# One band's PSUM read to ScalarE, the sums ahead of the differences' low halves on VectorE, and the row differences on GpSimd

## The chip, the core and the metric

One core of a Trainium2 chip runs the whole kernel. The metric is the device time of one execution in microseconds (us). TensorE (PE in the profile) multiplies, VectorE (DVE) and ScalarE (ACT) do the elementwise work and read PSUM, GpSimd (POOL) does elementwise work in SBUF, SyncE (SP) issues the transfers. PEld is TensorE's loading of weights.

## The reference, cut to what matters

The input is `x` of 8 images, 64 channels, 224 x 224, in fp32. With `g = _gn(x)` (group normalisation) the kernel returns

```python
res = conv3x3(g, W_id, b_id)                      # all 8 images: by far the largest part
out = leaky_relu(conv3x3(dmt, W_enc, b_enc), .01) # dmt comes from image 0 alone (wavelets, attention)
return x + (out + res)
```

`out` is one 64 x 224 x 224 map that is added to each image. The change concerns only `res` and the additions around it, which is the last stage of the kernel; the statistics, the wavelets and the `dmt` convolution run ahead of it.

## The kernel before

In the last stage an image is cut into an upper and a lower half, which lie on partitions 0 to 63 and 64 to 127, and each half into 14 bands of 8 rows. Of the 14 bands 7 are **direct** (a plain 3x3 convolution) and 7 are **minimal** (the F(2,3) scheme over rows, which makes two output rows from four products in place of six). Products run in fp16 with a high and a low half of each operand. That makes 56 direct bands and 56 minimal ones. The stage is written as 56 **rounds** `q`; in a round TensorE multiplies direct band `q+1` and minimal band `q` in turns, while the other engines prepare what the next rounds need. Each engine runs its list in order; semaphores join the lists.

TensorE's order in a round: `first_direct(q+1)`, `product_m2(q)`, `middle_direct(q+1)`, `product_m1(q)`, `last_direct(q+1)`, `product_m0(q)`, `product_m3(q)`, all on line L1766. `product_m0` waits for `b_seeded`, which VectorE's `seed_odd` gives.

What the names stand for, with the lines of the kernel before:

- `neighbour_sums(j)` (VectorE, L1928 and L1929): two operations of 896 columns on the raw band of minimal `j`; waits until that band's load has landed.
- `differences(j)` (VectorE, L1935): subtracts row r+2 from row r of that band in place, 1792 columns, fp32.
- `diffs_high` (ScalarE, L1863) and `diffs_low` (VectorE, L1946): high and low fp16 halves of the differences. `sums_high` (ScalarE, L1871) and `sums_low` (VectorE, L1940): the same for the sums.
- `high` and `full` (ScalarE, L1606 and L1612) and `split` (VectorE, L1619): the same for a direct band, 2240 columns.
- `read_direct(j, g)` (VectorE, L1954): reads bank pair `g` (0 or 1) of direct band `j` from PSUM into the stage for the store; `seed_direct` (ScalarE, L1633) then fills that bank for the next band. `seed_odd` (VectorE, L1961), `odd_rows` (VectorE, L1969), `even_rows` (ScalarE, L1886), `seed_minimal` (ScalarE, L1893) and `double` (ScalarE, L1879) do the minimal bands' work on PSUM.
- `build_part` (VectorE, L1734, L1738, L1743, L1745): makes half of the next image's weights. It runs in two of an image's seven rounds, for all images but the last: 14 **build rounds**.

The bands of `x` rotate through three buffers `xs`. SyncE's list in a round is: four stores of direct `q` (after both its banks are read), four stores of minimal `q-1`, then two loads of 560 KB each for direct `q+3`, then two for minimal `q+2`. A load waits for the buffer:

```python
def load(sp, k):
    ...
    if k >= XS:
        sp.wait_ge(split_done, k - XS + 1)
```

`split_done` is raised by `split` and by `diffs_low`. The load of minimal band `q+2` waits for `split(q+2)` in round `q`; the band is first read by `neighbour_sums(q+2)` in round `q+1`. GpSimd in this stage only fills border rows (L2019 and L2024).

Of the kernel before, what the change touches and what calls it, by code (L numbers as in the profile page):

```python
# [8 lines left out]
ALU = mybir.AluOpType  # L9
# [16 lines left out]
R = 8  # L26
NB = HALF // R
RH = R + 2
# [1417 lines left out]
def main(nc, x, t, out, ps, psum, sb, sem, top, pool_of, early, e_map, partner, mv_all, norm_all, w_max, unit):  # L1446
# [3 lines left out]
    with ExitStack() as s5:  # L1450
# [71 lines left out]
        banks_set = sem(top, "banks_set")  # L1522
        g_seeded = sem(top, "g_seeded")
        g_done = sem(top, "g_done")
        g_read = sem(top, "g_read")
        a_seeded = sem(top, "a_seeded")
        m2_done = sem(top, "m2_done")
        twice_ready = sem(top, "twice_ready")
# [30 lines left out]
        def place_w(j):  # L1559
            return min(2 * j + 2, ND + NW - 1)  # L1560
# [67 lines left out]
        def seed_direct(act, j, g):  # L1628

            i, b = direct(j)  # L1630
            if j:
                act.wait_ge(g_read, 2 * j - 1 + g)
            act.activation(g_bank[g], e_rows[:, :, b, g, :, :].rearrange("p r q w -> p r (q w)"), ACT.Identity,  # L1633
                           scale=lane(r_out, i), bias=lane(mean_r, i)).then_inc(g_seeded, 1)

# [192 lines left out]
        def sync(sp):  # L1828
            def store(i, b, p):
                for s in range(2):  # L1830
                    for k in range(2):
                        row0 = HALF * s + R * b + 4 * k
                        sp.dma_start(out[i, :, row0:row0 + 4, :].rearrange("c h w -> c (h w)"),
                                     stage[p][C * k:C * k + C, s, :, :].rearrange("c g n -> c (g n)")).then_inc(stored[p], 16)

            def store_direct(j):
                sp.wait_ge(g_read, 2 * j + 2)
                store(*direct(j), 0)

            def store_minimal(j):  # L1840
                sp.wait_ge(even_read, j + 1)
                sp.wait_ge(odd_read, 2 * j + 2)
                store(*minimal(j), 1)

            load(sp, 3)
            load(sp, 4)
            for q in range(NW):
                store_direct(q)
                if q:
                    store_minimal(q - 1)  # L1850
                load(sp, 2 * q + 5)
                load(sp, 2 * q + 6)
            store_minimal(NW - 1)
            for p in range(2):
                sp.wait_ge(stored[p], 64 * ND)

        def scalar(act):
            def diffs_high(j):
                i, b = minimal(j)
                act.wait_ge(diffs_ready, j + 1)  # L1860
                if j:
                    act.wait_ge(odd_done, j)
                act.activation(v_hi[:, 0:R, 1:1 + W], xs[place_w(j) % XS][:, 0:R * W].rearrange("p (r w) -> p r w", w=W), ACT.Identity,  # L1863
                               scale=norm_all[:, i, 0:1]).then_inc(diffs_hi, 1)

            def sums_high(j):
                i, b = minimal(j)
                act.wait_ge(sums_ready, j + 1)
                if j:
                    act.wait_ge(m1_done, j)  # L1870
                act.activation(v_hi[:, R:VR, 1:1 + W], sums.rearrange("p (r w) -> p r w", w=W), ACT.Identity,  # L1871
                               scale=norm_all[:, i, 0:1]).then_inc(sums_hi, 1)

            def double(j):
                i, b = minimal(j)
                act.wait_ge(m2_done, j + 1)
                if j:
                    act.wait_ge(b_seeded, j)
                act.activation(twice, a_bank, ACT.Identity, scale=-2.0, bias=lane(mean_r2, i)).then_inc(twice_ready, 1)  # L1879

            def even_rows(j):
                i, b = minimal(j)
                act.wait_ge(even_done, j + 1)
                if j:
                    act.wait_ge(stored[1], 64 * j)
                act.activation(stage[1][:, :, :, 0:W], a_bank.rearrange("p r (g w) -> p r g w", g=2), ACT.Identity,  # L1886
                               scale=lane(m_out, i)).then_inc(even_read, 1)

            def seed_minimal(j):
                i, b = minimal(j)  # L1890
                if j:
                    act.wait_ge(even_read, j)
                act.activation(a_bank.rearrange("p r (g w) -> p r g w", g=2), e_rows[:, :, b, :, 0, :], ACT.Identity,  # L1893
                               scale=lane(r_out, i), bias=lane(mean_r, i)).then_inc(a_seeded, 1)

            act.wait_ge(banks_set, 2)
            for q in range(-1, NW):
                if q >= 0:
                    diffs_high(q)
                if q >= 0 and q + 2 < ND:  # L1900
                    high(act, q + 2)
                if q >= 0:
                    double(q)
                if q >= 0 and q + 2 < ND:
                    full(act, q + 2)
                if q + 2 < ND:
                    seed_direct(act, q + 2, 0)
                if q + 1 < NW:
                    sums_high(q + 1)
                if q >= 0:  # L1910
                    even_rows(q)
                if q + 1 < NW:
                    seed_minimal(q + 1)
                if q + 2 < ND:
                    seed_direct(act, q + 2, 1)

        def vector(dve):
            def neighbour_sums(j):

                i, b = minimal(j)  # L1920
                k = place_w(j)
                landed(dve, k)
                if b == BOTTOM:
                    dve.wait_ge(filled, fill_of(i, b))
                v = xs[k % XS].rearrange("p (r w) -> p r w", w=W)
                odd, even = v[:, 1:R:2, :], v[:, 2:R + 1:2, :]
                half = [sums[:, CH * W * h:CH * W * h + CH * W].rearrange("p (r w) -> p r w", w=W) for h in range(2)]
                dve.scalar_tensor_tensor(half[0], odd, lane(neg_two, i), even, ALU.add, ALU.add)  # L1928
                dve.tensor_tensor(half[1], even, odd, ALU.subtract).then_inc(sums_ready, 1)  # L1929

            def differences(j):

                v = xs[place_w(j) % XS]
                dve.wait_ge(sums_ready, j + 1)
                dve.tensor_tensor(v[:, 0:R * W], v[:, 0:R * W], v[:, 2 * W:RH * W], ALU.subtract).then_inc(diffs_ready, 1)  # L1935

            def sums_low(j):
                i, b = minimal(j)
# [7 lines left out]
                dve.scalar_tensor_tensor(v_lo[:, 0:R, 1:1 + W], xs[place_w(j) % XS][:, 0:R * W].rearrange("p (r w) -> p r w", w=W),  # L1946
                                         norm_all[:, i, 0:1], v_hi[:, 0:R, 1:1 + W], ALU.mult, ALU.subtract).then_inc(split_done, 1)

            def read_direct(j, g):
                i, b = direct(j)  # L1950
                if j:
                    dve.wait_ge(stored[0], 64 * j)
                dve.wait_ge(g_done, 2 * j + g + 1)  # L1953
                dve.tensor_scalar(stage[0][:, :, g, :], g_bank[g], lane(m_out, i), None, ALU.mult).then_inc(g_read, 1)  # L1954

            def seed_odd(j):
                dve.wait_ge(m1_done, j + 1)
# [15 lines left out]
            for q in range(-1, NW):  # L1973
                if q > 0:
                    odd_rows(q - 1)
                if q >= 0:
                    diffs_low(q)
                if q + 1 < NW:
                    neighbour_sums(q + 1)
                i, b = direct(q + 1) if q + 1 < ND else (B, 0)  # L1980
                if i + 1 < B and b in DIRECT[2:4]:
                    build_part(dve, i + 1, DIRECT.index(b) - 2)
                if q + 1 < ND:
                    read_direct(q + 1, 0)
                if q >= 0 and q + 2 < ND:
                    split(dve, q + 2)
                if q >= 0:
                    seed_odd(q)
                if q + 1 < NW:
                    differences(q + 1)  # L1990
                    sums_low(q + 1)
                if q + 1 < ND:
                    read_direct(q + 1, 1)
            odd_rows(NW - 1)

        def tensor(pe):
# [14 lines left out]
        def gpsimd(pool):  # L2011
            for buf in (v_hi, v_lo):
                pool.memset(buf[:, :, 0:1], 0.0).then_inc(v_pads_set, 1)
                pool.memset(buf[:, :, WP - 1:WP], 0.0).then_inc(v_pads_set, 1)

            def fill_top(i):
                k = place_d(len(DIRECT) * i)
                pool.wait_ge(split_done, k - XS + 1)
                pool.memset(xs[k % XS][up, 0:W], 0.0).then_inc(filled, 1)  # L2019

            def fill_bottom(i):
                k = place_w(len(MINIMAL) * i + len(MINIMAL) - 1)
                pool.wait_ge(split_done, k - XS + 1)
                pool.tensor_copy(xs[k % XS][dn, (RH - 1) * W:RH * W], mean[dn, i:i + 1].broadcast_to((C, W))).then_inc(filled, 1)  # L2024

            for i in range(B):
                if i + 1 < B:
                    fill_top(i + 1)
                fill_bottom(i)

        ahead = Ahead(load=load, weights_load=weights_load, dummies=dummies, pads=pads, norms=norms, spread=spread, build=build,
                      normed=lambda act: act.wait_ge(normed, 1), high=high, full=full, split=split, edges=edges, root=root_of, partners=partners,
# [44 lines left out]
```

## Time and profile before

| | |
|---|---|
| time, median of 3 runs | 1817.76 us (1817.34 to 1818.57) |
| the profiled execution | 1814.87 us, its span 1813.1 us |
| mean granted TensorE clock | 0.994 |
| busy over the span: PE, DVE, ACT, POOL | 1761.4, 1450.2, 1238.6, 545.5 us |
| last stage, 1000 to 1100 us: PE, DVE, ACT, POOL busy | 99.19, 88.20, 73.18, 0.65 of 100 us |
| the same stretch: DMA engines busy, moved | 0.93, 240 GB/s |

The stage of the 56 rounds takes the span from about 812 us to its end. In it TensorE is nearly always busy, VectorE comes next, and GpSimd is idle. To read a round, take `even_rows` (L1886) as its mark: ScalarE always waits for TensorE there, so the distance from one L1886 to the next is the round's length. The profiled execution is 2.9 us faster than the median of the runs, 0.16%.

### The profile page before, as it was taken

To read this page: it belongs to the slowest core of one execution; us is meant where nothing else is said; L and a number is where in the kernel's file an instruction comes from. 1 tells how busy PE (TensorE), PEld (TensorE's weight loads), DVE (VectorE), ACT (ScalarE), POOL (GpSimd) and SP (SyncE) were. 2 spreads that over 40 slices of the span, in tenths; PEclk is the share of its full clock that TensorE was granted. 3 is DMA by queue.
4 is the path that set the end of the run, shared out by engine and by line. 5 is a ranking of instruction groups with operands and counts; after the bars stand their busy time and mean duration, and the time that the engine had idled before them with its cause. 6 is when DMAs were issued, how large, how long until landed. Compare 5 with 4: busy or idle time off the path is not lost. (4 is left out here: it accounts for less than half of the span.)

```text
span 1813.1 us, 69228 instructions
## 1 busy us (share of the span) xinstructions
PE 1761.4 (97%) x31540; PEld 1470.2 (81%) x31540; DVE 1450.2 (80%) x1926; ACT 1238.6 (68%) x1339; POOL 545.5 (30%) x365
## 2 busy tenths in 40 slices
PE   9999999999999999989999999999999999999997
PEld 9997999999999999965577797767966756967676
DVE  5665578778777887668989889888889888888886
ACT  5555666666666666667776777767776767766774
POOL 0005788888888888640000000000000000000000
PEclk9999999999999999999999999999999999999999
DMA  8884399888888888458998998998989989989994
GB/s 186 245 296 126 122 274 227 212 219 216 212 215 215 215 215 206 100 125 204 235 234 223 239 239 226 240 240 229 238 224 236 247 213 232 242 219 230 249 234 140
DMA packets 132964, 391.84 MB, mean 216 GB/s; under 512 B 49884, under 2 KB 50656, under 8 KB 118464
## 3 DMA queue, kind: packets, MB, share of 16 engines
q1 hardware_dynamic: 132672, 387.43, 82.7%
q8 instruction: 247, 4.05, 1.0%
q14 instruction: 45, 0.37, 0.1%
HBM read 258.88 MB, written 128.45 MB: 214 GB/s over the span
## 5 line engine op out<-in xcount | busy, mean ns | idle before, releaser
L1766 PE MATMUL ps<-big,tail 64*64 64x448 f16 x3840 | 323.3, 353 | 11.8 <-DVE ps L1961 7.8
L1766 PE MATMUL ps<-pool_of 64*64 64x448 f16 x5184 | 302.5, 352 | 7.9 <-DVE pool_of L1625 4.2
L1766 PE MATMUL ps<-pool_of,tail 64*64 64x448 f16 x4896 | 300.1, 349 | 0.7 <-issue 0.7
L1766 PE MATMUL ps<-big,pool_of 64*64 64x448 f16 x3552 | 278.5, 352 | 17.1 <-DVE ps L1961 11.9
L1292 DVE BATCH_NORM_STATS2 pool_of<-big 128x6 f32<-128x448 f32 x392 | 232.2, 616 | 76.4 <-DMA big<-in_x 76.3
L1766 PEld LDWEIGHTS ps<-pool_of 64*64 64x64 f16 x5184 | 196.2, 107 | 68.0 <-issue 10.1
L1766 PEld LDWEIGHTS ps<-pool_of,tail 64*64 64x64 f16 x4896 | 189.6, 106 | 59.3 <-issue 1.3
L1066 PE MATMUL ps<-pool_of 112*128 112x246 f16 x1344 | 218.8, 271 | 1.7 <-DVE pool_of L1280 0.8
L1070 PE MATMUL ps<-pool_of 112*128 112x168 f16 x1344 | 217.8, 243 | 0.0
L1766 PEld LDWEIGHTS ps<-big,tail 64*64 64x64 f16 x3840 | 169.0, 107 | 57.9 <-DVE ps L1961 10.4
L1069 PE MATMUL ps<-pool_of 112*128 112x90 f16 x1344 | 201.3, 206 | 0.0
L1766 PEld LDWEIGHTS ps<-big,pool_of 64*64 64x64 f16 x3552 | 134.3, 107 | 69.8 <-DVE ps L1961 15.8
L1886 ACT ACTIVATE tail<-ps,pool_of 128x896 f32<-128x896 f32 x56 | 56.5, 1008 | 180.8 <-PE ps L1766 180.8
L2019 POOL MEMSET pool_of<- 64x224 f32 x5 | 1.4, 277 | 558.5 <-DVE tail L1946 558.5
L1633 ACT ACTIVATE ps<-big,pool_of 128x896 f32<-128x896 f32 x112 | 122.5, 1095 | 55.0 <-DVE tail L1954 52.5
L1766 PE MATMUL ps<-tail 64*64 64x448 f16 x1344 | 155.5, 353 | 0.6 <-issue 0.6
L1100 PE MATMUL ps<-d_odd,shared 128*64 128x224 f16 x3024 | 148.1, 259 | 0.3 <-DVE pool_of L1280 0.3
L1100 PE MATMUL ps<-pool_of,shared 128*64 128x224 f16 x3024 | 148.3, 259 | 0.0
L628 PE MATMUL ps<-fh,pool_of 112*112 112x238 f32 (+1 forms) x512 | 144.3, 364 | 2.5 <-DVE big L860 1.3
L1100 PEld LDWEIGHTS ps<-d_odd,shared 128*64 128x64 f16 x3024 | 143.8, 110 | 2.6 <-issue 0.8
L1100 PEld LDWEIGHTS ps<-pool_of,shared 128*64 128x64 f16 x3024 | 143.8, 110 | 1.7 <-issue 0.2
L1766 PE MATMUL ps<-tail,pool_of 64*64 64x448 f16 x1344 | 143.5, 352 | 0.3 <-issue 0.3
(252 smaller groups left out, 3809.8 us busy)
## 6 DMA issues: line engine op xcount, KB each, us to landing
out<-tail SPq DMA_DIRECT2D x448, 224.0 KB, 3.6
big<-in_x SPq DMA_DIRECT2D x392, 224.0 KB, 5.2
pool_of<-in_x SPq DMA_DIRECT2D x139, 560.0 KB, 7.4
tail<-in_x SPq DMA_DIRECT2D x69, 560.0 KB, 7.4
pool_of<-row_filtered SPq DMA_DIRECT2D x110, 224.0 KB, 4.0
row_filtered<-big SPq DMA_DIRECT2D x2, 6272.0 KB, 22.8
pool_of<-in_x SPq DMA_DIRECT2D x30, 392.0 KB, 7.1
row_filtered<-big SPq DMA_DIRECT2D x4, 1568.0 KB, 9.2
```

What stands on the lines that cost most here:

```text
L628: pe.matmul(o[:, 0:width], xg[g][:, near, c % CG, :], fh[:, near, first:first + width], start=True, stop=False)
L1066: pe.matmul(tiles(o)[:, :, 15:NTILE], lhs[:, 1, a, :], tiles(v)[:, :, 15:NTILE], start=(k == 0), stop=False)
L1069: pe.matmul(tiles(o)[:, :, 0:15], lhs[:, 0, a, :], tiles(v)[:, :, 0:15], start=False, stop=False)
L1070: mm = pe.matmul(both(o), lhs[:, 0, a, :], both(v), start=False, stop=(k == 2))
L1100: mm = pe.matmul(o[s], weff[a][:, sw, i, ky, :], d[n][:, b, r:r + 4, sw, NTILE * i:NTILE * i + NTILE], start=(k == 0), stop=(k == len(piec ...
L1292: ins = dve.bn_stats(records[:, 2 * (k % CHN) + i, :], sx[k % 4][:, i * NT:i * NT + NT])
L1633: act.activation(g_bank[g], e_rows[:, :, b, g, :, :].rearrange("p r q w -> p r (q w)"), ACT.Identity, scale=lane(r_out, i), bias=lane(mean ...
L1766: mm = pe.matmul(psum[bank + r][C * k:C * k + C, 0:NT], wt[i % 2][lanes, h, s, kx, :], v[u][lanes, rows_of(k), kx:kx + W], start=False, st ...
L1886: act.activation(stage[1][:, :, :, 0:W], a_bank.rearrange("p r (g w) -> p r g w", g=2), ACT.Identity, scale=lane(m_out, i)).then_inc(even_ ...
L2019: pool.memset(xs[k % XS][up, 0:W], 0.0).then_inc(filled, 1)
```

## The change

Three edits in the last stage. The second bank's read moves from VectorE to ScalarE (`read_second`, behind `seed_minimal`), with a semaphore for each bank. On VectorE `neighbour_sums(q+1)` stands ahead of `diffs_low(q)`; it waits in addition for `sums_low` of the round before. `differences` moves from VectorE to GpSimd, which does one per round as soon as `neighbour_sums` is done, with the border fills between them.

```diff
-        g_read = sem(top, "g_read")
+        g_read = [sem(top, f"g_read{g}") for g in range(2)]
...
             if j:
-                act.wait_ge(g_read, 2 * j - 1 + g)
+                act.wait_ge(g_read[g], j)
...
             def store_direct(j):
-                sp.wait_ge(g_read, 2 * j + 2)
+                for g in range(2):
+                    sp.wait_ge(g_read[g], j + 1)
                 store(*direct(j), 0)
...
+            def read_second(j):
+                i, b = direct(j)
+                if j:
+                    act.wait_ge(stored[0], 64 * j)
+                act.wait_ge(g_done, 2 * j + 2)
+                act.activation(stage[0][:, :, 1, :], g_bank[1], ACT.Identity, scale=lane(m_out, i)).then_inc(g_read[1], 1)
...
                 if q + 1 < NW:
                     seed_minimal(q + 1)
+                if q + 1 < ND:
+                    read_second(q + 1)
                 if q + 2 < ND:
                     seed_direct(act, q + 2, 1)
...
                 i, b = minimal(j)
                 k = place_w(j)
+                if j:
+                    dve.wait_ge(sums_split, j)
                 landed(dve, k)
...
-            def differences(j):
-
-                v = xs[place_w(j) % XS]
-                dve.wait_ge(sums_ready, j + 1)
-                dve.tensor_tensor(v[:, 0:R * W], v[:, 0:R * W], v[:, 2 * W:RH * W], ALU.subtract).then_inc(diffs_ready, 1)
...
             for q in range(-1, NW):
                 if q > 0:
                     odd_rows(q - 1)
+                if q + 1 < NW:
+                    neighbour_sums(q + 1)
                 if q >= 0:
                     diffs_low(q)
-                if q + 1 < NW:
-                    neighbour_sums(q + 1)
                 i, b = direct(q + 1) if q + 1 < ND else (B, 0)
                 if i + 1 < B and b in DIRECT[2:4]:
                     build_part(dve, i + 1, DIRECT.index(b) - 2)
                 if q + 1 < ND:
-                    read_direct(q + 1, 0)
+                    read_first(q + 1)
                 if q >= 0 and q + 2 < ND:
                     split(dve, q + 2)
                 if q >= 0:
                     seed_odd(q)
                 if q + 1 < NW:
-                    differences(q + 1)
                     sums_low(q + 1)
-                if q + 1 < ND:
-                    read_direct(q + 1, 1)
...
+            def differences(j):
+
+                v = xs[place_w(j) % XS]
+                pool.wait_ge(sums_ready, j + 1)
+                pool.tensor_tensor(v[:, 0:R * W], v[:, 0:R * W], v[:, 2 * W:RH * W], ALU.subtract).then_inc(diffs_ready, 1)
+
+            for j in range(NW):
+                i, b = minimal(j)
+                if b == MINIMAL[-1]:
+                    pool.wait_ge(diffs_ready, j)
+                    fill_bottom(i)
+                    pool.wait_ge(filled, fill_of(i, b))
+                differences(j)
+                if b == MINIMAL[4] and i + 1 < B:
+                    pool.wait_ge(diffs_ready, j + 1)
                     fill_top(i + 1)
-                fill_bottom(i)
+                    pool.wait_ge(filled, fill_of(i + 1, TOP))
```

VectorE's list, one round without a build in the kernel before: `odd_rows` L1969, `diffs_low` L1946, `neighbour_sums` L1928 and L1929, the first bank's read L1954, `split` L1619, `seed_odd` L1961, `differences` L1935, `sums_low` L1940, the second bank's read L1954.

```order
L1969 SCALAR_TENSOR_TENSOR tail<-ps,pool_of,big 128x2x224 x2
L1946 SCALAR_TENSOR_TENSOR tail<-pool_of,norm_all,big 128x8x224
L1928 SCALAR_TENSOR_TENSOR pool_of<-tail,pool_of 128x896
L1929 TENSOR_TENSOR pool_of<-tail 128x896
L1954 TENSOR_SCALAR tail<-ps,pool_of 128x2x448
L1619 TENSOR_TENSOR big<-pool_of 128x10x224
L1961 TENSOR_TENSOR ps<-ps,pool_of 128x2x448
L1935 TENSOR_TENSOR tail<-tail 128x1792
L1940 SCALAR_TENSOR_TENSOR tail<-pool_of,norm_all,big 128x8x224
L1954 TENSOR_SCALAR tail<-ps,pool_of 128x2x448
```

The same round in the changed kernel, whose line numbers differ: `odd_rows` L1975, `neighbour_sums` L1940 and L1941, `diffs_low` L1952, the first bank's read L1960, `split` L1619, `seed_odd` L1967, `sums_low` L1946.

```order
L1975 SCALAR_TENSOR_TENSOR tail<-ps,pool_of,big 128x2x224 x2
L1940 SCALAR_TENSOR_TENSOR pool_of<-tail,pool_of 128x896
L1941 TENSOR_TENSOR pool_of<-tail 128x896
L1952 SCALAR_TENSOR_TENSOR tail<-pool_of,norm_all,big 128x8x224
L1960 TENSOR_SCALAR tail<-ps,pool_of 128x2x448
L1619 TENSOR_TENSOR big<-pool_of 128x10x224
L1967 TENSOR_TENSOR ps<-ps,pool_of 128x2x448
L1946 SCALAR_TENSOR_TENSOR tail<-pool_of,norm_all,big 128x8x224
```

The sums' two rows have moved ahead of `diffs_low`; the in-place subtraction of 1792 columns and the second bank's read are gone from this list. In a build round the four build lines stand directly behind `diffs_low` L1952, ahead of the first bank's read.

ScalarE's list around `even_rows` (L1887 now), one round of the changed kernel:

```order
L1887 ACTIVATE tail<-ps,pool_of 128x4x224
L1901 ACTIVATE ps<-big,pool_of 128x2x448
L1895 ACTIVATE tail<-ps,pool_of 128x2x448
L1633 ACTIVATE ps<-big,pool_of 128x2x448
L1864 ACTIVATE big<-pool_of,norm_all 128x8x224
L1606 ACTIVATE pool_of<-tail,norm_all 128x10x224
L1880 ACTIVATE pool_of<-ps,pool_of 128x896
L1612 ACTIVATE tail<-tail,norm_all 128x2240
```

Only L1895, `read_second`, is new; it stands ahead of `seed_direct` (L1633), `diffs_high` (L1864), `high`, `double` and `full`.

GpSimd's list in the stage, from its start: `differences` is L2033, the fills are L2022 and L2027.

```order
L2033 TENSOR_TENSOR tail<-tail 128x1792
L2033 TENSOR_TENSOR pool_of<-pool_of 128x1792 x2
L2033 TENSOR_TENSOR tail<-tail 128x1792
L2033 TENSOR_TENSOR pool_of<-pool_of 128x1792
L2022 MEMSET pool_of 64x224
L2033 TENSOR_TENSOR pool_of<-pool_of 128x1792
L2027 COPY tail<-pool_of 64x224
```

Before, this list held the fills alone; now there is one 1792-column subtraction with two inputs in SBUF per round.

## Rows read from the trace of the kernel before

**Rows 1.** Waits from 830 to 1794 us: waiter, releaser, total us, times, longest.

```profile
PEld ps L1766 <- DVE ps L1961: 23.7, 13, 2.4
PE ps L1766 <- DVE ps L1961: 18.1, 13, 2.0
```

**Rows 2.** ScalarE's timeline: start us, us, line, operation; in brackets the idle time before.

```profile
830.53 1.01 ACT L1886 ACTIVATE tail<-ps,pool_of 128x896 f32<-128x896 f32 x1 [2.71 <-PE ps L1766]
...
1047.46 1.01 ACT L1886 ACTIVATE tail<-ps,pool_of 128x896 f32<-128x896 f32 x1 [3.28 <-PE ps L1766]
...
1050.57 1.78 ACT L1863 ACTIVATE big<-pool_of,norm_all 128x1792 f16<-128x1792 f32 x1
...
1055.29 2.25 ACT L1612 ACTIVATE tail<-tail,norm_all 128x2240 f32<-128x2240 f32 x1
...
1064.56 1.01 ACT L1886 ACTIVATE tail<-ps,pool_of 128x896 f32<-128x896 f32 x1 [3.28 <-PE ps L1766]
...
1119.07 1.01 ACT L1886 ACTIVATE tail<-ps,pool_of 128x896 f32<-128x896 f32 x1 [2.58 <-PE ps L1766]
...
1794.19 1.01 ACT L1886 ACTIVATE tail<-ps,pool_of 128x896 f32<-128x896 f32 x1 [3.28 <-PE ps L1766]
```

**Rows 3.** VectorE's timeline in the round from 1047.46 us, which has no build.

```profile
1049.29 1.26 DVE L1969 SCALAR_TENSOR_TENSOR tail<-ps,pool_of,big 128x448 f32<-128x448 f32 x2
1052.38 2.09 DVE L1946 SCALAR_TENSOR_TENSOR tail<-pool_of,norm_all,big 128x1792 f16<-128x1792 f32 x1 [1.83 <-ACT big L1863]
1054.39 1.15 DVE L1928 SCALAR_TENSOR_TENSOR pool_of<-pool_of 128x896 f32<-128x896 f32 x1
1055.45 1.08 DVE L1929 TENSOR_TENSOR pool_of<-pool_of 128x896 f32<-128x896 f32 x1
1056.45 1.14 DVE L1954 TENSOR_SCALAR tail<-ps,pool_of 128x896 f32<-128x896 f32 x1
1057.64 2.50 DVE L1619 TENSOR_TENSOR big<-tail,pool_of 128x2240 f16<-128x2240 f32 x1
1060.05 1.09 DVE L1961 TENSOR_TENSOR ps<-ps,pool_of 128x896 f32<-128x896 f32 x1
```

**Rows 4.** One minimal band's load on SyncE; its landings; landings of all loads.

```profile
1043.43 1.11 SPq L1584 DMA_DIRECT2D pool_of<-in_x  x2
...
DMA to landing us min/median/max: 5.5/6.5/7.5
...
DMA to landing us min/median/max: 5.1/7.4/11.1
```

**Rows 5.** VectorE's and GpSimd's timelines ahead of the stage, 787 to 791 us.

```profile
788.59 2.42 DVE L1734 TENSOR_TENSOR pool_of<-pool_of 128x576 f32<-128x576 f32 x1
...
787.78 2.62 POOL L1396 TENSOR_TENSOR big<-big 128x896 f32<-128x896 f32 x1 [3.24 <-ACT big L1184]
```

**Rows 6.** The same two timelines, 809 to 811 us.

```profile
809.62 1.14 DVE L1954 TENSOR_SCALAR tail<-ps,pool_of 128x896 f32<-128x896 f32 x1
...
809.75 1.13 POOL L1392 TENSOR_TENSOR big<-big 128x448 f32<-128x448 f32 x1 [2.00 <-ACT big L1166]
```

**Rows 7.** The same two timelines, 1766 to 1770 us.

```profile
1766.92 1.15 DVE L1928 SCALAR_TENSOR_TENSOR pool_of<-tail,pool_of 128x896 f32<-128x896 f32 x1
1767.98 1.26 DVE L1929 TENSOR_TENSOR pool_of<-tail 128x896 f32<-128x896 f32 x1
...
1767.07 1.23 POOL L2024 COPY pool_of<-pool_of 64x224 f32<-64x224 f32 x1 [116.41 <-DVE tail L1946]
```

**Rows 8.** GpSimd's groups by shape over the span: count, busy us, mean ns.

```profile
L308 POOL TENSOR_TENSOR pool_of<-pool_of 112x1024 f32<-112x1024 f32 x55 | 130.2, 2367 | 0.0
...
L1384 POOL TENSOR_TENSOR big<-big,pool_of 128x224 f32<-128x224 f32 x84 | 53.0, 660 | 58.6 <-ACT big L1179 58.6
```

**Rows 9.** VectorE's timeline in the build round that ends at 1119.07 us.

```profile
1109.71 0.75 DVE L1734 TENSOR_TENSOR tail<-pool_of 128x576 f32<-128x576 f32 x1
...
1112.48 1.15 DVE L1954 TENSOR_SCALAR tail<-ps,pool_of 128x896 f32<-128x896 f32 x1 [0.22 <-DVEq L1747]
1113.55 2.48 DVE L1619 TENSOR_TENSOR pool_of<-tail,pool_of 128x2240 f16<-128x2240 f32 x1
```

More of the change, by code:

```diff
@@ L1947, in diffs_low, with read_first @@
                                          norm_all[:, i, 0:1], v_hi[:, 0:R, 1:1 + W], ALU.mult, ALU.subtract).then_inc(split_done, 1)
-            def read_direct(j, g):
+            def read_first(j):
                 i, b = direct(j)
@@ L1952, in read_direct @@
                     dve.wait_ge(stored[0], 64 * j)
-                dve.wait_ge(g_done, 2 * j + g + 1)
-                dve.tensor_scalar(stage[0][:, :, g, :], g_bank[g], lane(m_out, i), None, ALU.mult).then_inc(g_read, 1)
+                dve.wait_ge(g_done, 2 * j + 1)
+                dve.tensor_scalar(stage[0][:, :, 0, :], g_bank[0], lane(m_out, i), None, ALU.mult).then_inc(g_read[0], 1)
             def seed_odd(j):
@@ L2024, in fill_bottom @@
                 pool.tensor_copy(xs[k % XS][dn, (RH - 1) * W:RH * W], mean[dn, i:i + 1].broadcast_to((C, W))).then_inc(filled, 1)
-            for i in range(B):
-                if i + 1 < B:
+            def differences(j):
[11 more added lines that the diff above has]
+                    pool.wait_ge(diffs_ready, j + 1)
                     fill_top(i + 1)
-                fill_bottom(i)
+                    pool.wait_ge(filled, fill_of(i + 1, TOP))
         ahead = Ahead(load=load, weights_load=weights_load, dummies=dummies, pads=pads, norms=norms, spread=spread, build=build,
```

## The prediction

> **What bounds the kernel now.** I read the time by rounds. From the first `even_rows` to the last the stage takes 1794.19 − 830.53 = 963.66 us for 54 rounds [rows 2], 17.85 us each. A quiet round takes 1064.56 − 1047.46 = 17.1 us, and ScalarE waits 3.28 us for TensorE ahead of each mark [rows 2]: TensorE is the bound. The table of waits, next, shows what TensorE loses: 18.1 to 23.7 us in 13 waits for VectorE's `seed_odd` [rows 1], about one for each build round, where the build's operations push `seed_odd` back. That is nearly all that less work on VectorE can give back here: some 24 us of 1815. So I asked next what the moved work costs in its new places, and along which chain.
>
> **The change, part by part.** The second read on ScalarE costs about 1.0 us per round (as `even_rows`, 1.01 us [rows 2]); ScalarE idles 3.28 us per round, so the round is not longer for it. But it stands ahead of `diffs_high`, which before ended at 1050.57 + 1.78, 4.9 us after the mark; now 5.9. `full` ended 10.1 us after the mark (1055.29 + 2.25) and now ends at 11.1.
>
> VectorE loses one read, 1.14 us [rows 3], and the subtraction of 1792 columns.
>
> GpSimd gains that subtraction. None of this shape is in the trace. Its two-input operations take 660 ns for 224 columns and 2367 ns for 1024 [rows 8], 2.13 ns per column, so 2367 + 768 x 2.13 = 4.0 us. By itself that would be hidden: `diffs_high` needs it only in the next round.
>
> What it does to VectorE is the heart of the matter. At 788.59 VectorE began an L1734, fp32 with both inputs in SBUF. It took 2.42 us [rows 5]; the same line takes 0.75 elsewhere [rows 9]. Through that time GpSimd's L1396 ran until 790.40, and L1734 ended at 791.01: it stood still until GpSimd was done, and finished 0.61 us later, 0.14 less than its full length. A read from PSUM was not touched: L1954 beside a GpSimd addition took 1.14 us, its usual length, and the addition 1.13 [rows 6, 3]. So an operation of VectorE with two SBUF inputs and one of GpSimd take turns, whole instruction by whole instruction. The Trainium skill (SBUF — State Buffer, "Who interferes with whom") speaks against this change: VectorE's second SBUF input comes through a port pair that it shares with GpSimd, whoever starts first holds it for the whole instruction, and the other fully blocks. Taken to the letter, nothing of a blocked instruction is done early, which would put two times 0.14 us per round, 15 us in all, on the sum below; the row decides.
>
> In the changed round `neighbour_sums`, `diffs_low`, the build and `split` all read two SBUF inputs; only the first bank's read, `seed_odd` and `odd_rows` take one from PSUM. So 4.0 us per round close VectorE to most of its list, in the midst of it, where before 2.0 us were spent behind `seed_odd`, off the chain.
>
> Who goes first? `neighbour_sums` releases GpSimd, but VectorE's next operation starts 0.08 us before the last one ends (1054.39 against 1052.38 + 2.09 [rows 3]). In the one such meeting on record, GpSimd's L2024 was released and began at 1767.07; VectorE's L1928, begun at 1766.92, took its normal 1.15 us, and then L1929 took 1.26 in place of 1.08, until after GpSimd's end at 1768.30 [rows 7, 3]. So VectorE keeps the first place if it is ready, and GpSimd comes in at the next boundary of instructions. Is `diffs_low` ready? That depends on when the sums start, which brings in the loads.
>
> The sums move to a place directly behind `odd_rows`, 3.1 us after the mark (1049.29 + 1.26 − 1047.46), from 6.9 [rows 3]. Their band's load is issued when `split` of the round before ends. Of the pair at 1043.43 the second was issued 0.5 us behind the first and landed 7.5 us later, 8.0 after the pair began [rows 4]; a single transfer takes 5.1 to 11.1, median 7.4 [rows 4]. Before, these sums began at 1054.39, 3.0 us after that landing: covered. Now the cover is gone, and a ring closes from one `split` to the next:
>
> load 8.0, sums 2.14 (1054.39 to 1055.45 + 1.08), `diffs_low` 2.09 − 0.08 = 2.01, GpSimd's subtraction 4.0 − 0.14 = 3.86 (the first bank's read lies under it), `split` 2.50 − 0.14 = 2.36 [rows 3 to 5, 8]: **18.4 us**.
>
> A mark comes 3.04 us after the end of a `split` that TensorE waits for (1113.55 + 2.48 to 1119.07 [rows 9, 2]). So in this ring the sums end 8.0 + 2.14 − 3.04 = 7.1 us after the mark and `diffs_high` at 5.9: `diffs_low` is ready, goes first, and GpSimd second. In a build round the build stands behind `diffs_low` and is shut out too: 8.0 + 2.14 + 2.01 + 3.86 = 16.0, L1734's 0.61, then 1110.46 to 1116.03 = 5.57 for the rest of the build, the read and `split` [rows 9]: **22.2 us**.
>
> Sum: 40 x 18.4 + 14 x 22.2 = 1046.8 us in place of 963.66: +83 us. TensorE then waits 1.3 us or more in each round, so its present waits and short stops vanish in that. The profiled execution goes from 1814.87 to 1898. Its median lies 2.9 us above it, so 1901 as a median.
>
> Bounds. If each pair were down within the median of one transfer, 7.4 us, every round would give 0.6 back: −32. One microsecond more than 8.0, a third of the way to the longest row: +54. GpSimd's subtraction scaled by width alone from the 1024 columns would be 2367 x 1792 / 1024 = 4.1 us: +7; a fixed part larger than the 0.18 us of my line would take as much off: −7.
>
> The other waits that the change adds: that for `sums_low` stands behind it in VectorE's own list and is met. The direct band's stores now wait for ScalarE, 3.1 us after the mark (1.0 behind `seed_minimal`), and the next first read waits for them; it lies under GpSimd's 3.86 us with 2.8 to spare. GpSimd's list is empty when the sums end, but for fills of a few tenths in 15 of 56 rounds. So I cost these at nothing; without that cover the first read would put its own 1.07 us on the ring.
>
> **The rivals.**
>
> *GpSimd goes first.* If its release overtakes `diffs_low`, then sums 2.14, release 0.06, GpSimd 4.0, `diffs_low` 1.95, read 1.07, `split` 2.42 stand in a row behind the load: 8.0 + 11.64 = 19.6; with the build (2.69 between, then 3.55) 22.4. 40 x 19.6 + 14 x 22.4 − 963.7 = +134: about 1952. Against it speak [rows 7].
>
> *The loads don't limit.* If bands landed within about 6 us, the sums would start at 3.1 after the mark and end at 5.2, ahead of `diffs_high` (5.9). GpSimd goes first then, 9.2; `diffs_low` 11.15; read 12.2; `split` 14.65; mark 17.7. With the build 13.85, `split` 17.4, mark 20.4. 40 x 17.7 + 14 x 20.4 − 963.7 = +30: about 1848. No landing of a pair so short is in [rows 4], but the stage's loads meet less traffic when rounds get longer, so part of this way is possible.
>
> *The other side: faster.* If these two operations don't shut each other out, as those of [rows 6] don't, then GpSimd's 4.0 us are free. `split` ends at 11.1 + 2.4 = 13.5 (behind `full`), the load lands at 21.5, 4.4 into the next round, sums 6.5, `diffs_low` 8.5: a quiet round stays 17.1. A build round: 8.5 + 2.69 + 3.55 = 14.75, mark 17.8, so 0.7 late; the second in a row 1.25. That leaves 14 us of the 23.7 [rows 1]: 10 us gained, about 1808. It decides if VectorE's L1619 and L1952 keep their 2.5 and 2.1 us beside GpSimd. Against it speak [rows 5, 7]; for it only that the pair there was of other shapes.
>
> **How the numbers follow.** The ring with VectorE first 0.62 (1870 to 1935 by its bounds), GpSimd first 0.13, loads that don't limit 0.14, faster 0.08, no change to be seen 0.03 (if the ring comes out near 17.9 on the mean). I predict 1901. The range leaves out the faster case and no change, 0.11, and some of what lies above GpSimd's first place: 1838 to 1960. A measurement of this kernel can tell about 0.2%, 3.6 us, from no change: faster 0.08, within it 0.03, slower 0.89.
>
> **What would show it.** Right: GpSimd's L2033 busy near 4.0 us but shown longer, since it begins while `diffs_low` runs; `split` L1619 shown at 4 us or more in quiet rounds, and L1734 at over 3 in place of 0.75; `neighbour_sums` L1940 waiting for the load (a DMA as releaser) in most rounds; marks 18.4 and 22.2 us apart; TensorE waiting for `seed_odd` L1967 in all rounds, 60 us or more in sum; DMA below 0.93. Wrong: no wait of L1940 for a load (then the second rival), `diffs_low` L1952 stretched to 5 us or more in place of `split` (GpSimd first), or VectorE's operations at their old lengths (faster).

## The result and the profile after

The changed kernel takes 1933.42 us (median of 4 runs, 1928.34 to 1943.05) against 1818.16 us in the same runs: a ratio of 1.0641, 95% interval 1.0604 to 1.0678. It is slower by 115 us, inside the range and in the sense that was forecast, and by more than the 83 us of the sum. The profiled execution took 1928.34 us.

The page's first part, after: the span, then busy time of each engine. TensorE and VectorE have lost share, GpSimd has gained 295 us.

```profile
span 1926.6 us, 69361 instructions
PE 1789.5 (93%) x31540; PEld 1353.7 (70%) x31540; DVE 1419.5 (74%) x1814; ACT 1288.7 (67%) x1395; POOL 840.8 (44%) x421
```

ScalarE's timeline after, of `even_rows` (L1887 now), the marks of the rounds: the first, two neighbours of a quiet round, the end of the build round behind it, and the last that counts.

```profile
832.21 1.01 ACT L1887 ACTIVATE tail<-ps,pool_of 128x896 f32<-128x896 f32 x1 [3.89 <-PE ps L1766]
...
1656.05 1.01 ACT L1887 ACTIVATE tail<-ps,pool_of 128x896 f32<-128x896 f32 x1 [3.71 <-PE ps L1766]
...
1674.66 1.01 ACT L1887 ACTIVATE tail<-ps,pool_of 128x896 f32<-128x896 f32 x1 [4.79 <-PE ps L1766]
...
1699.08 1.01 ACT L1887 ACTIVATE tail<-ps,pool_of 128x896 f32<-128x896 f32 x1 [4.24 <-PE ps L1766]
...
1907.29 1.01 ACT L1887 ACTIVATE tail<-ps,pool_of 128x896 f32<-128x896 f32 x1 [3.29 <-PE ps L1766]
```

The 54 rounds take 1907.29 − 832.21 = 1075.08 us, in place of 963.66 [rows 2]: 111.4 of the 113.5 us by which the profiled executions differ. By all the marks the 40 quiet rounds are 18.8 us each on the mean (median 18.6), the 14 build rounds 23.0 (median 23.1).

The table of waits from 830 to 1900 us (waiter, releaser, total us, times, longest):

```profile
PEld ps L1766 <- DVE ps L1967: 124.7, 50, 6.1
PE ps L1766 <- DVE ps L1967: 103.2, 50, 5.6
...
DVE pool_of L1940 <- DMA pool_of<-in_x: 57.6, 26, 3.6
...
DVE pool_of L1940 <- DMA tail<-in_x: 28.6, 12, 3.3
```

TensorE waits for `seed_odd` (L1967) in 50 rounds where it did in 13 [rows 1], 103 to 125 us in place of 18 to 24. The sums (L1940) wait for a load in 38 rounds, which no row of before shows.

The ring that the prediction foretold, a loop of waits from one `split` to the next, can be read off one quiet round. The timeline after, piece by piece: SyncE's pair of loads, VectorE, GpSimd, and SyncE's next pair.

```profile
1653.06 1.11 SPq L1584 DMA_DIRECT2D pool_of<-in_x  x2
...
1661.25 1.15 DVE L1940 SCALAR_TENSOR_TENSOR pool_of<-pool_of 128x896 f32<-128x896 f32 x1 [2.20 <-DMA pool_of<-in_x]
1662.32 1.08 DVE L1941 TENSOR_TENSOR pool_of<-pool_of 128x896 f32<-128x896 f32 x1
1663.32 2.08 DVE L1952 SCALAR_TENSOR_TENSOR tail<-tail,norm_all,big 128x1792 f16<-128x1792 f32 x1
1665.32 1.15 DVE L1960 TENSOR_SCALAR tail<-ps,pool_of 128x896 f32<-128x896 f32 x1
1667.26 4.38 DVE L1619 TENSOR_TENSOR pool_of<-pool_of 128x2240 f16<-128x2240 f32 x1 [0.80 <-ACT pool_of L1612]
...
1663.49 5.80 POOL L2033 TENSOR_TENSOR pool_of<-pool_of 128x1792 f32<-128x1792 f32 x1 [12.82 <-DVE pool_of L1941]
...
1671.67 1.11 SPq L1584 DMA_DIRECT2D pool_of<-in_x  x2
```

The view of line L1584 after, in the window of the first pair, gives the time from each issue to its landing:

```profile
DMA to landing us min/median/max: 6.2/6.9/7.6
```

The second load lands about 1653.6 + 7.6 = 1661.2, the sums begin at 1661.25 and end at 1663.40. `diffs_low` is ready and goes first, to 1665.40, at its usual 2.08 us. GpSimd's L2033, shown from 1663.49, ends at 1669.29: 3.89 us behind `diffs_low`. The read from PSUM (L1960) lies under it at its usual length. `split` L1619 is shown from 1667.26 but ends at 1671.64, 2.35 behind GpSimd, and at 1671.67 the next load is issued: 18.61 us from pair to pair. So an instruction that waits for the other engine is shown as a long one, from where it began to wait.

The build round that follows, VectorE and GpSimd after:

```profile
1682.46 2.08 DVE L1952 SCALAR_TENSOR_TENSOR tail<-pool_of,norm_all,big 128x1792 f16<-128x1792 f32 x1
1684.46 4.56 DVE L1734 TENSOR_TENSOR tail<-pool_of 128x576 f32<-128x576 f32 x1
...
1691.91 2.48 DVE L1619 TENSOR_TENSOR big<-tail,pool_of 128x2240 f16<-128x2240 f32 x1
...
1682.62 5.78 POOL L2033 TENSOR_TENSOR pool_of<-pool_of 128x1792 f32<-128x1792 f32 x1 [13.34 <-DVE pool_of L1941]
```

GpSimd ends at 1688.40, 3.86 us behind `diffs_low`; L1734, which took 0.75 [rows 9], takes 4.56 and ends 0.62 behind GpSimd; `split` ends at 1694.39. The next mark is at 1699.08, 4.69 us later, where the sum had 3.04. The view by windows (us, busy time and count of PE, PEld, DVE, ACT, POOL, then the granted clock as a share of 2.4 GHz, DMA share, GB/s) gives the clock for the quiet round and for the stretch behind this `seed_odd`:

```profile
1656.00:1674.00 18.00, 16.69 (x353) 10.19 (x348) 13.24 (x10) 13.76 (x10) 5.80 (x1) 1.00 0.88 218
...
1695.40:1702.00 6.60, 6.55 (x95) 3.41 (x97) 2.72 (x3) 2.88 (x3) 0.00 (x0) 0.66 0.79 174
```

TensorE had waited 5.4 us for this `seed_odd`. Behind it the granted clock is 0.66 on the mean of 6.6 us: by slices of 1 us it is 0.50, the lower of its two levels (1.2 GHz), until 1699.4, and 1.00 (2.4 GHz) from 1700.4. From `seed_odd`'s end to the mark takes 3.5 to 3.7 us in 11 of the 14 build rounds, where 2.0 us are usual.

### The profile page after: what moved, and what is told of

The parts are those of the page before. It is cut to its first block and busy times, and to the rows that moved or that the text cites. A ratio compares the mean times of both kernels' runs of the same rounds, so it can differ in the third digit from the quotient of the medians.

```text
span 1926.6 us, 69361 instructions
## 1 busy us (share of the span) xinstructions
PE 1789.5 (93%) x31540; PEld 1353.7 (70%) x31540; DVE 1419.5 (74%) x1814; ACT 1288.7 (67%) x1395; POOL 840.8 (44%) x421
## 5 line engine op out<-in xcount | busy, mean ns | idle before, releaser
L2033 POOL TENSOR_TENSOR pool_of<-pool_of 128x1792 f32<-128x1792 f32 x37 | 194.3, 5252 | 436.2 <-DVE pool_of L1941 435.8
L1766 PE MATMUL ps<-big,tail 64*64 64x448 f16 x3840 | 304.6, 363 | 51.1 <-DVE ps L1967 49.0
L1766 PE MATMUL ps<-pool_of 64*64 64x448 f16 x5184 | 294.4, 351 | 8.4 <-DVE pool_of L1625 4.2
L1766 PE MATMUL ps<-pool_of,tail 64*64 64x448 f16 x4896 | 291.4, 349 | 1.9 <-issue 1.8
L1766 PEld LDWEIGHTS ps<-pool_of 64*64 64x64 f16 x5184 | 157.0, 107 | 102.3 <-issue 6.4
L1887 ACT ACTIVATE tail<-ps,pool_of 128x896 f32<-128x896 f32 x56 | 56.4, 1008 | 244.0 <-PE ps L1766 237.8
L1766 PEld LDWEIGHTS ps<-big,tail 64*64 64x64 f16 x3840 | 122.0, 110 | 134.2 <-DVE ps L1967 59.7
L1766 PEld LDWEIGHTS ps<-pool_of,tail 64*64 64x64 f16 x4896 | 152.0, 106 | 85.8 <-issue 1.3
L1766 PEld LDWEIGHTS ps<-big,pool_of 64*64 64x64 f16 x3552 | 109.1, 110 | 136.8 <-DVE ps L1967 66.6
L2033 POOL TENSOR_TENSOR tail<-tail 128x1792 f32<-128x1792 f32 x19 | 99.2, 5221 | 221.9 <-DVE pool_of L1941 221.8
L1633 ACT ACTIVATE ps<-big,pool_of 128x896 f32<-128x896 f32 x112 | 122.9, 1098 | 82.0 <-DVE tail L1960 79.9
L1975 DVE SCALAR_TENSOR_TENSOR tail<-ps,pool_of,big 128x448 f32<-128x448 f32 x112 | 71.4, 679 | 133.0 <-PE ps L1766 133.0
```

The lines of the kernel that those rows point to most:

```text
L1766: mm = pe.matmul(psum[bank + r][C * k:C * k + C, 0:NT], wt[i % 2][lanes, h, s, kx, :], v[u][lanes, rows_of(k), kx:kx + W], start=False, st ...
L1975: dve.scalar_tensor_tensor(stage[1][:, r, :, W:NT], b_bank[:, r, :].rearrange("p (g w) -> p g w", g=2), lane(m_out, i), e_rows[:, r, b, :, ...
L2033: pool.tensor_tensor(v[:, 0:R * W], v[:, 0:R * W], v[:, 2 * W:RH * W], ALU.subtract).then_inc(diffs_ready, 1)
```

## The experiments

All ratios are to the kernel before on the same chip, with 95% intervals. Times of the 54 rounds are from mark to mark in the profiled executions.

**The subtraction back on VectorE**, in VectorE's list as before, and out of GpSimd's (the first two edits alone):

```diff
                 if q >= 0:
                     seed_odd(q)
                 if q + 1 < NW:
+                    differences(q + 1)
                     sums_low(q + 1)
```

> The subtraction goes back to VectorE, behind seed_odd; the second read on ScalarE and the sums ahead of diffs_low stay. Theory (turn-taking between GpSimd's subtraction and VectorE's two-input operations closes the ring): split back at 2.5 us, quiet rounds 17.1 us, build rounds 0.7 and 1.25 us above that, about 1808 us. Rival (the loss is the sums' earlier place alone, which takes the cover from the loads): the sums still wait for their loads each round and the time stays over 1860 us.

Measured: 1832.52 us, ratio 1.0062 (1.0047 to 1.0077). So 101 of the 115 us go with the subtraction alone, and `split` is back at 2.5 us. But 1808 was missed: the two other edits are no gain, they cost 0.6%. The table of waits, 830 to 1780 us, shows the sums waiting for loads in this kernel too, in 44 rounds:

```profile
DVE pool_of L1940 <- DMA pool_of<-in_x: 86.0, 30, 5.1
...
DVE pool_of L1940 <- DMA tail<-in_x: 35.6, 14, 4.0
```

The build rounds took 266 us in all, as before; the quiet ones 17.9 us each on the mean where before took 17.4. In the 11 quiet rounds of more than 18 us the sums begin 5.2 to 8.1 us after the mark. The rival is right in that the exposure exists and wrong in its size.

**The subtraction alone on GpSimd** (out of VectorE's list, into GpSimd's):

```diff
-                    differences(q + 1)
...
+                pool.wait_ge(sums_ready, j + 1)
+                pool.tensor_tensor(v[:, 0:R * W], v[:, 0:R * W], v[:, 2 * W:RH * W], ALU.subtract).then_inc(diffs_ready, 1)
```

> The kernel before with the subtraction alone moved to GpSimd. Theory: diffs_low ends 7.0 us after the mark, the sums 9.1, GpSimd 13.1, split 15.5, the next mark 18.5; with a build 22.3; so 40 x 18.5 + 14 x 22.3 = 1052 us for the 54 rounds, about 1907 us in all, and no sums that wait for a load. Rival of the loads alone: no load is exposed, about 1818 us. Rival that only GpSimd's slowness counts (its result comes late): diffs_high needs it a round later, so about 1818 us too.

Measured: 1927.93 us, ratio 1.0593 (1.0576 to 1.0610). Both rivals fall. The median quiet round is 18.5 us, as worked out, the build round 23.3 against 22.3. In build rounds `seed_odd`'s end to the mark takes up to 3.7 us again, and here the ring runs through the mark (the mark, `diffs_high`, `diffs_low`, the sums, GpSimd, `split`), so that this lengthens it. VectorE's and GpSimd's timelines in a quiet round and in a build round:

```profile
1663.14 1.14 DVE L1948 TENSOR_SCALAR tail<-ps,pool_of 128x896 f32<-128x896 f32 x1
1664.33 5.36 DVE L1619 TENSOR_TENSOR pool_of<-pool_of 128x2240 f16<-128x2240 f32 x1
...
1663.31 4.03 POOL L2023 TENSOR_TENSOR pool_of<-pool_of 128x1792 f32<-128x1792 f32 x1 [14.52 <-DVE pool_of L1929]
...
1541.59 0.75 DVE L1734 TENSOR_TENSOR tail<-pool_of 128x576 f32<-128x576 f32 x1
1542.38 3.90 DVE L1738 SCALAR_TENSOR_TENSOR tail<-pool_of,tail 128x64 f32<-128x64 f32 x1
...
1541.75 4.45 POOL L2023 TENSOR_TENSOR pool_of<-pool_of 128x1792 f32<-128x1792 f32 x1 [14.53 <-DVE pool_of L1929]
```

In the quiet round VectorE reads PSUM while GpSimd works, then stands in `split` until 1667.34. In the build round L1734 follows the sums at once, gets the first place, and GpSimd comes in behind it; then L1738, an operation of 64 columns, takes 3.90 us.

**GpSimd writes and reads nothing** (the differences are left out):

```diff
-                pool.tensor_tensor(v[:, 0:R * W], v[:, 0:R * W], v[:, 2 * W:RH * W], ALU.subtract).then_inc(diffs_ready, 1)
+                pool.memset(v[:, 0:R * W].bitcast(F16), 0.0).then_inc(diffs_ready, 1)
```

> The changed kernel, in which GpSimd fills the band with zeros (3584 fp16 columns) in place of subtracting: it writes the same bytes and reads nothing; the differences are left out of the computation. From its fill of 672 fp16 columns in 656 ns I estimate 3.5 us. Theory, in its form that what is shared is the way by which a second input is read: VectorE keeps its lengths beside the fill, split 2.5 us, time 1805 to 1820 us. If GpSimd shuts VectorE out whatever it does, split stays at 4 us or more and the time over 1880 us. If GpSimd's slowness alone counts, over 1880 us as well, but with split at 2.5 us.

Measured: 1831.83 us, ratio 1.0063 (1.0047 to 1.0079), the same as with the subtraction on VectorE. The groups by line (count, busy us, mean ns):

```profile
L2033 POOL MEMSET pool_of<- 128x3584 f16 x36 | 111.1, 3085 | 449.3 <-DVE pool_of L1941 449.0
L1952 DVE SCALAR_TENSOR_TENSOR tail<-pool_of,norm_all,big 128x1792 f16<-128x1792 f32 x36 | 74.9, 2081 | 0.0
...
L1619 DVE TENSOR_TENSOR big<-pool_of 128x2240 f16<-128x2240 f32 x18 | 44.8, 2487 | 2.3 <-ACT pool_of L1612 2.2
...
L1734 DVE TENSOR_TENSOR tail<-pool_of 128x576 f32<-128x576 f32 x14 | 10.5, 751 | 0.0
```

GpSimd's fill takes 3.1 us in the same place (0.9 less than the subtraction). In most quiet rounds it is over before `split` begins, so `split`'s 2.49 us say little; the witnesses are `diffs_low` (L1952), which lies beside the fill in 48 rounds, and L1734, in all 14 builds: both keep their lengths, 2.08 and 0.75 us, and so does the fill. It isn't GpSimd's being busy or late that costs, but its reading SBUF against a second SBUF input of VectorE. That is the line which the Trainium skill draws (SBUF — State Buffer, "Who interferes with whom": such a VectorE instruction contends with a GpSimd instruction that reads SBUF, not with one that only writes it), and these runs agree with it on both sides. The fill is another kind of operation than the subtraction, and one on GpSimd with a single SBUF input was not tried. The time missed its window, which ended at 1820; the sums wait for their loads in 44 rounds here too.

**The sums back behind `diffs_low`**, the rest as changed:

```diff
-                if q + 1 < NW:
-                    neighbour_sums(q + 1)
                 if q >= 0:
                     diffs_low(q)
+                if q + 1 < NW:
+                    neighbour_sums(q + 1)
```

> The changed kernel with the sums put back behind diffs_low; the loads are covered again, the subtraction stays on GpSimd and the second read on ScalarE. Theory: diffs_low ends 8.0 us after the mark, the sums 10.1, GpSimd 14.1, split 16.5, next mark 19.5; with a build 23.4; 40 x 19.5 + 14 x 23.4 = 1108 us, about 1962 us, slower than the changed kernel. Rival of the loads alone: the cover is back, 1815 to 1840 us.

Measured: 1998.98 us, ratio 1.0987 (1.0964 to 1.1009): the slowest of all, as only the theory had it, though 37 us above its figure. The median quiet round is 19.6 us (19.5 expected), the build round 24.5 (23.4). So the second edit, which exposes the loads, wins 3% back here: with the sums early, GpSimd's turn ends 13.2 us after the mark in the median round, against 14.2 in this run.

**The same subtraction on GpSimd, later**:

```diff
-                pool.wait_ge(sums_ready, j + 1)
+                pool.wait_ge(sums_split, j + 1)
```

> The changed kernel with GpSimd's subtraction released by sums_low in place of the sums: the same work on GpSimd, begun about half a microsecond ahead of the next mark, when VectorE's list comes to a read from PSUM and a wait. Theory (what costs is that the two meet, and what stands behind): 4.0 us per round on GpSimd stay, split and the build fall back to 2.5 and 0.75 us, and only the loads' exposure that showed without any subtraction on GpSimd remains, +0.4 to +1.0% over the kernel before (1825 to 1838 us). Rival (work on GpSimd slows VectorE wherever it lies): 1880 us or more.

Measured: 1833.28 us, ratio 1.0110 (1.0076 to 1.0145); of the 115 us some 100 are gone by one changed wait. Groups by line:

```profile
L2033 POOL TENSOR_TENSOR pool_of<-pool_of 128x1792 f32<-128x1792 f32 x36 | 144.5, 4014 | 465.5 <-DVE tail L1946 465.5
...
L1619 DVE TENSOR_TENSOR pool_of<-pool_of 128x2240 f16<-128x2240 f32 x18 | 44.8, 2488 | 4.1 <-ACT pool_of L1612 4.1
...
L1734 DVE TENSOR_TENSOR tail<-pool_of 128x576 f32<-128x576 f32 x14 | 10.5, 751 | 0.0
```

The work is all there, 4.01 us each, and all three lines have their undisturbed lengths.

**Half of each minimal band loaded** (5 of 10 rows; the rest of the buffer keeps old values, which stand in for the missing rows):

```diff
+                if k and k % 2 == 0 and k >= XS:
+                    hi_row = 5
```

> The changed kernel with half of each minimal band loaded, 5 of its 10 rows (the rest of the buffer keeps what it held): this leaves out a quarter of the stage's loads, and the bands land earlier. Theory: the load's part of the ring shrinks until it no longer limits, GpSimd goes first and the rounds go to 17.7 us, 21.4 with a build and its slower clock; 40 x 17.7 + 14 x 21.4 = 1008 us, about 1863 us (1850 to 1885). If the load were no part of the ring, 1925 us or more.

Measured: 1870.04 us, ratio 1.0287 (1.0273 to 1.0302): 63 us less than the changed kernel. The median quiet round is 17.9 us (17.7 expected), the build round 21.6 (21.4). The loads' part of the ring is real, and with less of it the ring through `odd_rows`, GpSimd and `split` stands near the 17.7 us that the second rival had worked out.

**The read alone, and the sums alone**, each in the kernel before:

```diff
-                    read_direct(q + 1, 1)
...
+                    read_second(q + 1)
```

> The kernel before with the second bank's read alone moved to ScalarE. Theory: diffs_high and so diffs_low end 1.0 us later, split 13.7 and seed_odd 14.6 us after the mark, in time for a round of 17.1; with a build the mark comes at 19.4, where it came at 18.1 and 19.3; about 1824 us (1818 to 1830). Rival (it takes work from the engine that TensorE waits for): 1800 us.

Measured: 1829.27 us, ratio 1.0058 (1.0036 to 1.0080). The build rounds are 19.4 us in the median, as worked out: the read delays `diffs_high` by its own microsecond, and `diffs_low` with it (it waits for `diffs_high` 2.8 us a round in place of 1.7), which costs more than it takes from VectorE. The quiet rounds together take 10 us more than before, for which nothing was worked out. The rival's 1800 us falls.

```diff
+                if j:
+                    dve.wait_ge(sums_split, j)
...
-                if q >= 0:
-                    diffs_low(q)
                 if q + 1 < NW:
                     neighbour_sums(q + 1)
+                if q >= 0:
+                    diffs_low(q)
```

> The kernel before with the sums alone ahead of diffs_low. If the exposure of the loads is what cost 0.6% in the kernel with the first two edits, it shows here too: the sums wait for their load in most rounds, and the time is 1825 us or more. If the two edits cost only together (the read puts ScalarE a microsecond later, and split with it, and the load is issued later), 1812 to 1822 us: split then waits for full at 10.1 us after the mark in quiet rounds, and a build round gains some tenths.

Measured: 1824.31 us, ratio 1.0036 (1.0021 to 1.0052). The sums wait for loads, 63.4 us in 31 rounds on one buffer's name and 31.7 in 15 on the other; the build rounds take 261.5 us in place of 266, the quiet ones 709.9 in place of 697.6. The time lies between the two expectations, so this run does not tell them apart: that the sums' new place costs a little by itself is shown, and that loads are exposed in it; that the exposure grows with the read is not.

**The build at the end of VectorE's round**, in the kernel before, an edit that the waits of [rows 1] suggest:

```diff
-                i, b = direct(q + 1) if q + 1 < ND else (B, 0)
-                if i + 1 < B and b in DIRECT[2:4]:
-                    build_part(dve, i + 1, DIRECT.index(b) - 2)
...
                 if q + 1 < ND:
                     read_direct(q + 1, 1)
+                i, b = direct(q + 1) if q + 1 < ND else (B, 0)
+                if i + 1 < B and b in DIRECT[2:4]:
+                    build_part(dve, i + 1, DIRECT.index(b) - 2)
```

> The kernel before with one edit of another kind: build_part moves from its place ahead of the first bank's read to the end of VectorE's round. Theory (the kernel before lost time to VectorE only through the build ahead of seed_odd): the 18 to 24 us of TensorE's waits for seed_odd go to 0 to 4, about 1798 us. Rival (VectorE's load of 15.6 us and 2.7 more per build round is too much wherever it lies): the waits move to the next round, 1812 to 1820 us.

Measured: 1790.40 us, ratio 0.9848 (0.9834 to 0.9861): faster than both kernels. TensorE's waits for `seed_odd` fall from 13 to 2, 1.6 us in all. ScalarE's marks around a build round whose build lies at its end, and around the next, are 17.1 us apart, the length of a quiet round:

```profile
1441.06 1.01 ACT L1886 ACTIVATE tail<-ps,pool_of 128x896 f32<-128x896 f32 x1 [3.28 <-PE ps L1766]
...
1458.15 1.01 ACT L1886 ACTIVATE tail<-ps,pool_of 128x896 f32<-128x896 f32 x1 [3.28 <-PE ps L1766]
...
1475.26 1.01 ACT L1886 ACTIVATE tail<-ps,pool_of 128x896 f32<-128x896 f32 x1 [3.28 <-PE ps L1766]
```

**The build last together with the later subtraction**: the read on ScalarE, the subtraction on GpSimd released by `sums_low`, the sums behind `diffs_low`, the build last.

> The second read on ScalarE and the subtraction on GpSimd, but released by sums_low, the sums behind diffs_low as before, the build at the end of VectorE's round. Theory: no load is exposed, GpSimd's 4.0 us meet a read from PSUM and a wait in quiet rounds; in build rounds they meet the build, whose lateness of up to 4 us is covered by the wait for diffs_high; 1795 to 1805 us, not measurably better than the build moved alone. If the meeting with the build is not covered: 1815 us or more.

Measured: 1812.37 us, ratio 0.9972 (0.9961 to 0.9982), 7 to 17 us above what was expected, just short of the 1815 of its rival, and 22 us behind the build moved alone. GpSimd meets the build in VectorE's timeline:

```profile
1488.23 4.11 DVE L1738 SCALAR_TENSOR_TENSOR tail<-pool_of,tail 128x64 f32<-128x64 f32 x2
...
1487.61 4.46 POOL L2033 TENSOR_TENSOR pool_of<-pool_of 128x1792 f32<-128x1792 f32 x1 [13.45 <-DVE tail L1946]
```

That makes the round behind the second build about 18.1 us in place of 17.1, some 7 us in all. The 54 rounds together take 956.7 us, 20 more than with the build moved alone; the other 13 I have not traced to a cause.

## Why the prediction was right, and by how much it was short

*Turn-taking.* Right, and the step that carries the forecast. VectorE's operations with two SBUF inputs and GpSimd's subtraction exclude each other: L1734 at 4.56 us, L1738 at 3.90, `split` at 4.38 and 5.36 in the rounds shown; with writes alone on GpSimd, or with the same work at another time, all are back. The price, 4.0 − 0.14 = 3.86 us, was 3.86 and 3.89 in the two rounds shown, and the subtraction undisturbed takes 4.01 where 4.0 were worked out from two other shapes. `split` too ends 2.35 us behind GpSimd in place of 2.49, so the 0.14 us that the sum took off at each of the two meetings are there.

*Who goes first.* Right in 45 of the 54 rounds, where `diffs_low` kept its 2.1 us; in the others the load was in time, the sums ended before `diffs_high`, and GpSimd went first, with `diffs_low` at 5.1 to 5.7 us. These are mostly the second build rounds. Eight of the nine follow a mark that came late, 4.2 to 4.7 us behind `split`'s end, so that their load landed early in the round. The prediction had this order as the second rival's, with "part of this way is possible", but its sum has no term for a mixture of the two.

*The ring by the loads.* Right in kind: the sums wait for their load in 38 rounds, and with shorter loads the quiet round shrinks to 17.9 us, near the 17.7 of the second rival. As to size, 18.4 us was worked out for a quiet round, and the median is 18.6, the mean 18.8. The sum has 8.0 us from `split`'s end to the sums' start; in the 38 rounds in which the sums waited for their load it is 8.6 in the median, from 7.7 to 10.0, and the ring passes each microsecond on. The 8.0 came from a single pair of loads, and the bound of one microsecond more covers the mean of the rounds. That bound gives +54, which would put the upper end of "1870 to 1935" at 1955; the measured 1933 lies within both.

*The sum.* 1046.8 us were worked out and 1075.1 measured, 28 us short. The term that was mis-sized is the load's 8.0 us. The ring closes from one `split` to the next, so it is best read there: the 52 rounds between the first `split`'s end and the last's took 1036.1 us, where the sum has 39 x 18.4 + 13 x 22.2 = 1006.2. Of these 30 us 24 lie between a `split`'s end and the sums' start, 8.46 us on the mean. About 4 more come from a term put at nothing, GpSimd's fills: in 7 rounds L2022 waits for `diffs_low` and stands ahead of the subtraction, which then ends 4.5 us behind `diffs_low` in place of 3.87.

The clock had no term either. In 11 of 14 build rounds the way from `split`'s end to the mark took 4.5 to 4.7 us in place of 3.04, as TensorE now waits 5 us where it had waited 2 in the round from which the 3.04 was taken. But the next load is issued at `split`'s end and not at the mark, so most of that delay is no loss: the next interval between marks is shorter by it. The rounds behind the first two second builds took 18.4 and 18.3 us by the marks, but 19.2 and 19.1 from `split` to `split`; there the sums began behind the late `odd_rows` and not behind their load, which is a few of the 24 us. In the kernel with the subtraction alone on GpSimd the ring runs through the mark, and there the build rounds are 1 us longer than worked out.

*What was costed at nothing.* I wrote that with the read on ScalarE "the round is not longer for it". In the changed kernel the later `diffs_high` is covered by the loads; alone the read costs 0.6%. The faster rival, 1808 us, has the later `diffs_high` and `full` in it, and what failed there is the load's time again: it lets the sums begin 4.4 us after the mark, and in the kernel without the exclusion they begin at 5.8 on the mean and at up to 8.1, so quiet rounds don't stay at 17.1 and the kernel takes 1832.

*The shares don't add.* Alone, the edits cost 0.6, 0.4 and 5.9%, together 6.4, the first and third without the second 9.9. The second edit is a loss by itself and a gain beside the other two, where it moves GpSimd's turn forward. The read costs 0.6% by itself and 3.7% more beside the third edit alone (1998.98 us against 1927.93), where the ring runs through `diffs_high`.

## What to carry to other kernels

Before work goes to GpSimd, list which operations VectorE runs in that time and how many of their inputs lie in SBUF; here an idle engine's microseconds were free beside reads of PSUM and where VectorE waited anyway. A wait that starts GpSimd later, and not less work, was worth 100 us here. And where VectorE is said to be the bound, look at which of its operations stands ahead of the one that is waited for: moving the build behind it gave 28 us, and taking 3 us per round off VectorE gave none (1833 us with the subtraction later on GpSimd).

## What the runs showed of the hardware that was not expected

A blocked instruction counts as busy in the profile: GpSimd's 4.0 us are shown as 5.8 when they queue behind `diffs_low`, and `split`'s 2.5 as 4.4. VectorE's busy time fell by only 31 us although 56 subtractions and 56 reads left it, some 177 us by [rows 3] and the subtraction's 2.0 us. TensorE's clock was granted at 0.66 over 6.6 us right behind a wait of 5.4 us, in a stage that before ran at 0.99; and what that costs hangs on the ring: little where the next load starts at `split`'s end, 1 us per build round where the ring runs through the mark.
